# Four-layer graph kernel on one core: layer 0's one-hot matrices and gathered adjacency kept in DRAM and loaded again in layer 3, instead of being computed a second time

## The chip, the cores and the metric

One core of a Trainium2 chip runs the whole kernel. The metric is the device time of one execution in microseconds (us). Engines are named as the profile names them: PE is TensorE (PEld its weight loads), DVE is VectorE, ACT is ScalarE, POOL is GpSimd, SP is SyncE, whose queue (SPq) issues most transfers.

## What is computed

`x` is 2048 x 128, `adj` a 2048 x 2048 matrix of zeros and ones with a density of about 0.001 (some two ones in a row). Before every layer x is normalised and passed through a ReLU (`h`), and each layer's result is added to x.

```python
# layer 0: attention with 4 heads, softmax over the neighbours
e = leaky_relu(parent[:, None, :] + child[None, :, :], 0.2)
att = softmax(where(adj[..., None] > 0, e, -9e15), axis=1)
x = x + einsum('njh,jhf->nhf', att, wh).reshape(n, -1)
# layer 1: adj.T @ h, divided by the degree; layer 2: Chebyshev terms of adj, two products
# layer 3
XW = h @ W;  den = exp(leaky_relu(s_row[:, None] + s_col[None, :], 0.01))
num = adj @ den
att = where(num != 0, den / where(num != 0, num, 1), 0)
x = x + adj @ (att @ XW)
```

## The kernel before, in words

A tile is 128 of the 2048 nodes, so there are T = 16 tiles of nodes `it`, and each adjacency column block has 16 row blocks `jt`. The adjacency lies in SBUF in bf16, as `A` and turned as `AT`. Since a tile of 128 nodes has few distinct neighbours, layers 0 and 3 don't multiply by full columns: for each tile the neighbours are numbered (slots, `slotb`), in three chunks of row blocks (`CHUNKS` = 0 to 5, 6 to 12, 13 to 15), and a one-hot matrix `G` (128 x 16 x 128, bf16, 512 KB) picks them out. A matmul with G gathers the neighbours' rows, of AT among others. The adjacency gathered so is called `ATc` in layer 0 (3 chunks, 128 x 384) and `ATc3` in layer 3.

Each of these two layers first reads a flag that DVE computed (`dense`, `dense3`) and takes a branch (`choose`, L352): `by_slots`, which runs here, or `over_all`. Every engine does this by itself. The flag costs a register load and a jump.

Layer 0 by slots, per tile (`by_slots` of each engine): DVE writes G in one instruction (`one_hot`, L1517), PE gathers from it (`gather`, L1010: 48 matmuls with the node features at L1019, 16 with AT at L1021), ACT copies the two results out of PSUM (`slot_copies`, L680: wc and ATc), DVE makes 12 weight blocks `zc` out of them (`slot_weights`, L1527), PE multiplies these (`slot_output`, L1026). SP brings a row of thresholds per tile (`rows`, 256 KB, L433). G and ATc have two buffers, wc and zc four. DVE's order is one_hot(it+1), slot_weights(it).

Layers 1 and 2 are three dense products (L1059, L1081) with conversions and joins beside them. Before layer 2's last product is joined, DVE makes the first two one-hots of layer 3 (L1614, L1619) and clears a small matrix `Eb`.

Layer 3 by slots. PE works in this order for tile it (`tile3`): num3(it, 0) (L1224, L1231), u3(it-1, 0 and 1) (L1242), num3(it, 1), u3(it-1, 2 and 3), then gather3(it+2) (L1194): 16 matmuls of G3 with AT, one with Eb (which puts a one in a place of the gathered adjacency for nodes that have no neighbours), and 16 of G3 with the six columns of `rp`. ACT takes a logarithm and an exponential per quarter (L843, L845) and copies ATc3 (L851). DVE's order for tile it is one_hot3(it+2) and then, for each of four quarters c, a row block of denominators for tile it+1 (`den3`, L1736, three of them, and `own3`, L1745, in the fourth), times_y (L1754), times_own (L1761), refine (L1768); after the third quarter edges3(it+2) (L1723 to L1727), which reads what gather3(it+2) left. num3(it+1, 0) waits for all three den3 of tile it+1. So PE and DVE each have a fixed order and hand over to each other a few times per tile. All engines loop twice over buffers b = 0 and 1 (`sweep`), with the first two and last two tiles written out.

At layer 3's start PE does gather3(0), t_row(2), gather3(1), t_row(3) (a t_row, L1141, spreads a row of factors over all partitions), and ACT copies each t_row (L796) before it goes to layer 3's branch.

Of the kernel before, what the change touches and what calls it, by code (L numbers as in the profile page):

```python
# [31 lines left out]
P = 128  # L32
# [3 lines left out]
H = 4  # L36
# [24 lines left out]
def gnn_stack(nc, x, adj, w0, att0, w2, w3, a3, out):  # L61
    ctx = ExitStack()
    with ctx:
# [43 lines left out]
        ATc = [at(f"ATc_{b}", B + 39 + 0.75 * b, [P, NC, P], BF16) for b in range(2)]  # L107
        rows = [at(f"rows_{b}", B + 44 + 2 * b, [P, H * P]) for b in range(2)]
        tauT = at("tauT", B + 42.5, [T * H, P])
        tau = nc.dram_tensor("tau", (T * H, P), F32).ap()  # L110
        rest0 = at("rest0", B + 52, [P, 4, WC])
# [49 lines left out]
        Eb = at("Eb", 176, [P, T, P], BF16)  # L161
# [15 lines left out]
        def const(name, shape, dt=F32):  # L177
            size = 1
            for n in shape[1:]:
# [15 lines left out]
        mk = const("mk", [P, T])  # L195
        over3 = const("over3", [P, 1])
# [77 lines left out]
        rows_loaded = [sem(f"rows_loaded{b}") for b in range(2)]  # L274
        pc_ready = sem("pc_ready")
# [3 lines left out]
        g3_ready = sem("g3_ready")  # L279
# [3 lines left out]
        at3_ready = sem("at3_ready")  # L283
# [60 lines left out]
                  g3_used: 2, e3_copied: 2, at3_ready: 2, num3_bank: 8, acc_used: 2, t_ready: 4, att3_ready: 8, att3_used: 8, un3_kept: 2,  # L344
# [68 lines left out]
        def _(sp):  # L413
# [22 lines left out]
            choose(sp, 0, by_slots, lambda: None)  # L436
# [8 lines left out]
        def _(pool):  # L445
# [163 lines left out]
        def _(act):  # L609
# [71 lines left out]
            def slot_copies(it, b):  # L681
# [4 lines left out]
                act.wait_ge(pc_ready, it + 3)  # L686
                nc.scalar.copy(ATc[b % 2][:, :, :].rearrange("p c i -> p (c i)"),
# [13 lines left out]
            def by_slots():  # L701
                rounds(act, slot_copies, previous_output)
                copy_output(T - 1)
                act.sem_inc(bc_copied, 48)
# [100 lines left out]
            def over_all3():  # L805
                broadcast_copies(52)
# [40 lines left out]
            def edges3(it, b):  # L847

                act.wait_ge(g3_used, it + 3)
                act.wait_ge(num3_bank, 4 * it + 4)  # L850
                nc.scalar.copy(ATc3[b][:, :, :].rearrange("p c i -> p (c i)"), bank[4 + b][:, 0:NC * P]).then_inc(at3_ready, 1)  # L851

# [8 lines left out]
            def tile3(it, b):  # L861
# [4 lines left out]
                if within(it, 2):  # L866
                    edges3(it + 2, b)

            def by_slots3():
                act.wait_ge(rp_ready, 10)  # L870
                edges3(0, 0)
                edges3(1, 1)
# [8 lines left out]
        def _(pe):  # L881
# [160 lines left out]
            def by_slots():  # L1042
                pe.wait_ge(pieces0_ready, 25)
                gather(0, 0)
# [150 lines left out]
            def gather3(it, b):  # L1195


                pe.wait_ge(g3_ready, 2 * it + 2)
                pe.wait_ge(e3_copied, it + 1)
                pe.wait_ge(at3_ready, it + 1)  # L1200
                for c, (first, end) in enumerate(CHUNKS):
                    for jt in range(first, end):
                        nc.tensor.matmul(bank[4 + b][:, P * c:P * c + P], G3[b][:, jt, :],
                                         AT[:, jt, bass.ds(it * P, P)], start=jt == first, stop=jt == end - 1 and c > 0)
                    if c == 0:
                        nc.tensor.matmul(bank[4 + b][:, 0:P], Eb[:, bass.ds(it, 1), :].rearrange("p o s -> p (o s)"),
                                         identb[:, :], start=False, stop=True)
                    for jt in range(first, end):
                        last = nc.tensor.matmul(bank[4 + b][:, P * NC + 6 * c:P * NC + 6 * c + 6], G3[b][:, jt, :],
# [4 lines left out]
            def num3(it, b, p):  # L1214
# [3 lines left out]
                pe.wait_ge(at3_ready, it + 3)  # L1218
# [36 lines left out]
            def by_slots3():  # L1255
                pe.wait_ge(rp_ready, 10)
# [13 lines left out]
        def _(dve):  # L1270
# [182 lines left out]
            def finish(o):  # L1453
# [5 lines left out]
                                             ALU.subtract))  # L1459
                then(nc.vector.tensor_tensor(Os[:, :, :, :], tcol[:, :, :].unsqueeze(3).to_broadcast([P, T, H, F1]),  # L1460
# [57 lines left out]
            def one_hot(it, b):  # L1518

                dve.wait_ge(gathered, it + 1)  # L1520
                if not isinstance(it, int):
                    apart(dve)
                nc.vector.tensor_tensor(G[b % 2][:, :, :], iota[:, :].unsqueeze(1).to_broadcast([P, T, P]),  # L1523
                                        slotb[:, bass.ds(it, 1), :].rearrange("p o j -> p (o j)").unsqueeze(2)
                                        .to_broadcast([P, T, P]), ALU.is_equal).then_inc(g_ready, 1)

            def slot_weights(it, b):  # L1527
# [5 lines left out]
                for c in range(NC):  # L1533
                    for h in range(H):
                        last = nc.vector.scalar_tensor_tensor(  # L1535
                            zc[b][:, c, h, :], rows[b % 2][:, P * h:P * h + P],
                            wc[b][:, c, H * F1 + h:H * F1 + h + 1], ATc[b % 2][:, c, :], ALU.max, ALU.mult)
                last.then_inc(pc_ready, 1)

            def by_slots():  # L1540
                one_hot(0, 0)
                for it in range(T):
                    if it + 1 < T:
                        one_hot(it + 1, (it + 1) % 4)
# [64 lines left out]
            def one_hot3(it, b):  # L1609

# [224 lines left out]
```

## Time and profile before

| | us |
|---|---|
| median of 3 runs | 692.52 |
| lowest and highest | 686.78, 692.58 |
| the profiled execution, whole | 690.29 |
| its span, first to last instruction | 688.5 |

What lies around the span is 1.8 us. The page gives PE 83% busy, DVE 72%, ACT 36% and POOL 13% of the span, but these are averages over stages. By the timeline the stages are: loading and turning the adjacency up to 72 us, layer 0 by slots from 72 to 201, layers 1 and 2 up to about 376, layer 3 by slots from 376 to 652, its last dense product up to the end. Each place below is given in us from the span's start.

### The profile page before, as it was taken

To read this page: it belongs to the slowest core of one execution; us is meant where nothing else is said; L and a number is where in the kernel's file an instruction comes from. 1 tells how busy PE (TensorE), PEld (TensorE's weight loads), DVE (VectorE), ACT (ScalarE), POOL (GpSimd) and SP (SyncE) were. 2 spreads that over 40 slices of the span, in tenths; PEclk is the share of its full clock that TensorE was granted. 3 is DMA by queue.
4 is the path that set the end of the run, shared out by engine and by line. 5 is a ranking of instruction groups with operands and counts; after the bars stand their busy time and mean duration, and the time that the engine had idled before them with its cause. 6 is when DMAs were issued, how large, how long until landed. Compare 5 with 4: busy or idle time off the path is not lost.

```text
span 688.5 us, 15070 instructions
## 1 busy us (share of the span) xinstructions
PE 569.2 (83%) x5741; PEld 519.8 (76%) x5741; DVE 497.5 (72%) x1001; ACT 250.0 (36%) x401; POOL 89.0 (13%) x81
## 2 busy tenths in 40 slices
PE   1688589999902998598897499999999899999797
PEld 1577589999901565497884299999899899998697
DVE  2853498888385355446767399999999999999611
ACT  2699011121003133365544123433333333333363
POOL 1119000000010001243432000000000000002041
PEclk9995699999755999699998699999999999999999
DMA  8693111111000000000000000000000000000001
GB/s 299 262 371 144 38 48 48 34 44 46 0 1 0 1 1 0 0 1 1 1 1 2 3 1 2 2 1 0 0 0 0 0 0 0 0 1 1 0 17 46
DMA packets 8355, 24.37 MB, mean 35 GB/s; under 512 B 688, under 2 KB 3696, under 8 KB 6256
## 3 DMA queue, kind: packets, MB, share of 16 engines
q1 hardware_dynamic: 7328, 23.10, 9.3%
q10 hardware_dynamic: 976, 0.59, 0.3%
q8 instruction: 32, 0.52, 0.3%
q14 instruction: 19, 0.16, 0.1%
HBM read 22.61 MB, written 1.08 MB: 34 GB/s over the span
## 4 chain that ended last, share of the span: by engine, by line
PE 43%; DVE 17%; issue 6%; ACT 4%; POOL 1%; DVEq 0%; ACTq 0%; POOLq 0%
PE bank L1224 15%; PE bank L1081 10%; PE bank L1059 7%; PE bank L1231 4%; PE bank L1242 4%; DVE h L1345 2%; DVE denw L1736 2%; DVE dTc L1761 2%; DVE tc L1754 2%; ACT yc L843 2%; DVE yc L1768 1%; ACT yc L845 1%; PE bank L1111 1%; DVE stats L1299 1%; DVE e L1643 1%
## 5 line engine op out<-in xcount | busy, mean ns | idle before, releaser
L1224 PE MATMUL bank<-ATc,denc 128*128 128x128 f32 x1024 | 122.5, 278 | 19.5 <-DVE denw L1736 18.6
L1224 PEld LDWEIGHTS bank<-ATc,denc 128*128 128x128 f32 x1024 | 118.1, 194 | 21.9 <-issue 18.9
L1081 PE MATMUL bank<-pcs,Ar 128*128 128x256 f32 x768 | 95.1, 287 | 7.2 <-DVEq L1331 3.7
L1081 PEld LDWEIGHTS bank<-pcs,Ar 128*128 128x128 f32 x768 | 93.9, 196 | 8.8 <-DVEq L1331 4.7
L843 ACT ACTIVATE yc<-bank 128x512 f32<-128x512 f32 x64 | 37.7, 589 | 155.5 <-PE bank L1231 155.5
L537 POOL CAST Ar<-AT 128x2048 fp32r<-128x2048 bf16 x24 | 47.4, 1984 | 312.8 <-PE bank L1231 245.1
L1019 PE MATMUL bank<-whp,G 128*128 128x136 bf16 x768 | 63.1, 226 | 8.9 <-DVE G L1523 8.9
L1242 PE MATMUL bank<-XW,yc 128*128 128x128 f32 x512 | 67.0, 285 | 2.6 <-DVE yc L1768 2.6
L1059 PE MATMUL bank<-pcs,A 128*128 128x385 bf16 x256 | 45.4, 339 | 28.7 <-DVEq L1324 28.7
L1242 PEld LDWEIGHTS bank<-XW,yc 128*128 128x128 f32 x512 | 60.8, 195 | 6.7 <-DVE yc L1768 3.0
L1535 DVE SCALAR_TENSOR_TENSOR zc<-rows,wc,ATc 128x128 f32<-128x128 f32 x192 | 51.8, 347 | 18.7 <-ACT wc L685 18.7
L1019 PEld LDWEIGHTS bank<-whp,G 128*128 128x128 bf16 x768 | 56.4, 101 | 9.1 <-issue 6.1
L1059 PEld LDWEIGHTS bank<-pcs,A 128*128 x256 | 25.8, 101 | 47.8 <-issue 31.7
L1021 PE MATMUL bank<-AT,G 128*128 (+1 forms) x256 | 56.8, 222 | 0.0
L1038 PE MATMUL bank<-wc,zc 128*128 128x33 f32 x384 | 49.7, 290 | 0.9 <-ACT Oc L694 0.9
L1038 PEld LDWEIGHTS bank<-wc,zc 128*128 128x128 f32 x384 | 48.6, 208 | 1.1 <-issue 1.1
L730 ACT CAST Ar<-AT 128x2048 fp32r<-128x2048 bf16 x24 | 45.5, 1907 | 0.0
L1754 DVE TENSOR_TENSOR tc<-bank,yc 128x512 f32<-128x512 f32 x64 | 43.8, 684 | 1.9 <-ACT yc L845 1.2
L1761 DVE TENSOR_TENSOR dTc<-dTc,yc 128x512 f32<-128x512 f32 x64 | 44.7, 699 | 0.0
L1736 DVE TENSOR_SCALAR denc<-cB,rc 128x2048 f32<-128x2048 f32 x32 | 42.9, 1342 | 0.3 <-DVE rc L1727 0.3
L1768 DVE SCALAR_TENSOR_TENSOR yc<-tc,dTc 128x512 f32<-128x512 f32 x64 | 42.5, 684 | 0.0
L845 ACT ACTIVATE yc<-yc 128x512 f32<-128x512 f32 x64 | 40.4, 631 | 2.0
(202 smaller groups left out, 793.6 us busy)
## 6 DMA issues: line engine op xcount, KB each, us to landing
a<-in_adj SPq DMA_DIRECT2D x16, 1024.0 KB, 6.1
rows<-tau SPq DMA_DIRECT2D x16, 256.0 KB, 3.2
out<-X SPq DMA_DIRECT2D x4, 256.0 KB, 2.2
W<-in_L_gnn_W ACTq DMA_DIRECT2D x1, 192.0 KB, 6.5
attB<-in_L_gnn_att_weight ACTq DMA_DIRECT2D x1, 128.0 KB, 4.7
a3B<-in_L_gnn_a ACTq DMA_DIRECT2D x1, 128.0 KB, 8.9
W<-in_L_gnn_weight ACTq DMA_DIRECT2D x1, 64.0 KB, 1.9
W<-in_L_gnn_W ACTq DMA_DIRECT2D x1, 64.0 KB, 6.9
```

The costliest lines, as they stand in the source:

```text
L843: nc.scalar.activation(yc[b][c][:, :], bank[c][:, :], ACT.Ln).then_inc(ln_ready, 1)
L1019: nc.tensor.matmul(bank[b % 2][:, WC * c:WC * c + WC], G[b % 2][:, jt, :], whp[:, jt, k, :], start=jt == first and k == 0, stop=jt == end ...
L1021: last = nc.tensor.matmul(bank[2 + b % 2][:, P * c:P * c + P], G[b % 2][:, jt, :], AT[:, jt, bass.ds(it * P, P)], start=jt == first, stop= ...
L1038: last = nc.tensor.matmul(bank[7][:, F1 * h:F1 * h + F1], zc[b][:, c, h, :], wc[b][:, c, F1 * h:F1 * h + F1], start=c == 0, stop=c == NC - 1)
L1059: last = nc.tensor.matmul(bank[b][:, 0:columns], adjacency[:, kt, bass.ds((GT * q + 2 * g + b) * P, P)], pieces[:, kt, 0:columns], start=k ...
L1081: last = nc.tensor.matmul(bank[t % 2][:, 0:2 * D], Ar[t % 4][:, kt, :], pieces[:, kt, :], start=kt == 0, stop=kt == T - 1)
L1224: nc.tensor.matmul(bank[c][:, P * k:P * k + P], denc[b][:, part, j0:j0 + P], ATc3[b][:, part, :], start=k == 0 and part == 0, stop=False, ...
L1242: last = nc.tensor.matmul(bank[6 + b][:, 0:D], yc[b][c][:, P * k:P * k + P], XW[:, 4 * c + k, 0:D], start=c == 0 and k == 0, stop=c == 3 a ...
L1535: last = nc.vector.scalar_tensor_tensor(zc[b][:, c, h, :], rows[b % 2][:, P * h:P * h + P], wc[b][:, c, H * F1 + h:H * F1 + h + 1], ATc[b ...
L1736: nc.vector.tensor_scalar(den, row[:, :], rc[b][:, c, 0:1], rc[b][:, c, 1:2], ALU.mult, ALU.max).then_inc(denc_ready, 1)
L1754: nc.vector.tensor_tensor(tc[c % 2][:, :], bank[c][:, :], yc[b][c][:, :], ALU.mult).then_inc(t_ready, 1)
L1761: nc.vector.tensor_tensor(own, own, yc[b][c][:, :], ALU.mult).then_inc(yd_ready, 1)
```

## The change

In layer 0, SP stores each G (512 KB) and each ATc to DRAM (`kept_G`, `kept_A`). ATc is now f32 (192 KB instead of 96). G takes layer 3's form in layer 0 already: its last chunk is written by a second instruction, so that both halves of its 128 columns hold the same 64 slots. Therefore `slot_weights` writes only the upper half of partitions in the last chunk, and POOL clears the lower halves of the four zc buffers once, with four memsets inside its branch, for which PE waits. After layer 0, SP overwrites one row in each tile of kept_A (`lone`, 2048 single words), which takes the place of Eb. The first two one-hots are made by DVE before its branch. The two tiles that layer 3 starts with are loaded into G3 and ATc3 during the dense layers, the others inside layer 3 by SP. Layer 3's one-hots, the 17 matmuls that gathered AT, Eb and ACT's copies into ATc3 are gone.

```diff
 # SP, layer 0, per tile (rows as before, then)
+                    keep_one_hot(it)
+                    if it > 0:
+                        keep_adjacency(it - 1)
+                keep_adjacency(T - 1)
...
+            def keep_one_hot(it):
+                sp.wait_ge(g_ready, 2 * it + 2)
+                sp.dma_start(kept_G[P * it:P * it + P, :], G[it % 2][:, :, :].rearrange("p j s -> p (j s)")
+                             ).then_inc(g_kept[it % 2], 16)
+            def keep_adjacency(it):
+                sp.wait_ge(e_copied, it + 3)
+                sp.dma_start(kept_A[P * it:P * it + P, :], ATc[it % 2][:, :, :].rearrange("p c i -> p (c i)")
+                             ).then_inc(a_kept[it % 2], 16)
+            def fetch(it):
+                b = it % 2
+                if it >= 2:
+                    sp.wait_ge(g3_used, it + 1)
+                sp.dma_start(G3[b][:, :, :].rearrange("p j s -> p (j s)"), kept_G[P * it:P * it + P, :]
+                             ).then_inc(g3_loaded[b], 16)
+                if it >= 2:
+                    sp.wait_ge(num3_bank, 4 * it + 4)
+                sp.dma_start(ATc3[b][:, :, :].rearrange("p c i -> p (c i)"), kept_A[P * it:P * it + P, :]
+                             ).then_inc(a3_loaded[b], 16)
 # POOL, layer 0, inside its branch
+                for b in range(4):
+                    nc.gpsimd.memset(zc[b][0:HP, NC - 1, :, :], 0.0).then_inc(zc_zero, 1)
 # ACT, slot_copies of layer 0, ahead of the copy to ATc
+                if within(it, -2):
+                    act.wait_ge(a_kept[b % 2], 8 * (it - b % 2))
 # PE, layer 0, before its first gather
+                pe.wait_ge(zc_zero, 4)
 # PE, gather3
-                pe.wait_ge(g3_ready, 2 * it + 2)
+                pe.wait_ge(g3_loaded[b], 8 * (it - b) + 16)
                 pe.wait_ge(e3_copied, it + 1)
-                pe.wait_ge(at3_ready, it + 1)
...
-                        nc.tensor.matmul(bank[4 + b][:, P * c:P * c + P], G3[b][:, jt, :],
-                                         AT[:, jt, bass.ds(it * P, P)], start=jt == first, stop=jt == end - 1 and c > 0)
 # DVE, one_hot of layer 0
+                if it >= 2:
+                    dve.wait_ge(g_kept[it % 2], 16 * (it // 2))
 # DVE, ahead of layer 0's branch
+            dve.wait_ge(choice, 1)
+            one_hot(0, 0)
+            one_hot(1, 1)
             choose(dve, 0, *counted(by_slots, over_all))
 # DVE, tile3 of layer 3
-                if within(it, 2):
-                    one_hot3(it + 2, b)
```

How the instructions move, at the three places that matter. First PE in layer 3, the end of the order for tile 0 and the start of tile 1 (`denc`, `denw` are the denominators of num3, `AT` the adjacency). Before:

```order
L1224 MATMUL bank<-ATc_0_185,denc_159 128x128 x16
L1231 MATMUL bank<-ATc_0_185,denw_161 128x128 x8
L1203 MATMUL bank<-AT,G_0_166 128x128 x6
L1206 MATMUL bank<-identb,Eb 128x128
L1209 MATMUL bank<-rp,G_0_166 128x6 x6
L1203 MATMUL bank<-AT,G_0_166 128x128 x7
L1209 MATMUL bank<-rp,G_0_166 128x6 x7
L1203 MATMUL bank<-AT,G_0_166 128x128 x3
L1209 MATMUL bank<-rp,G_0_166 128x6 x3
L1224 MATMUL bank<-ATc_1_186,denc_160 128x128 x16
```

The same place on PE after the change:

```order
L1277 MATMUL bank<-ATc_0_184,denc_159 128x128 x16
L1284 MATMUL bank<-ATc_0_184,denw_161 128x128 x8
L1262 MATMUL bank<-rp,G_0_166 128x6 x16
L1277 MATMUL bank<-ATc_1_185,denc_160 128x128 x16
L1284 MATMUL bank<-ATc_1_185,denw_162 128x128 x8
```

Of 33 matmuls between the two num3, the 17 with 128 columns went and the 16 with six columns stayed.

Second DVE in layer 3, the end of tile 1 and the start of the loop with tile 2 (ISA rows are register work of the loop). Before:

```order
L1768 SCALAR_TENSOR_TENSOR yc_174<-tc_187,dTc_165 128x512
L1768 SCALAR_TENSOR_TENSOR yc_175<-tc_188,dTc_165 128x512
L368 UNCONDITIONAL_BRANCH
L368 ISA
L1614 ISA
L1614 TENSOR_TENSOR G_0_166<-iota,slotb 128x1664
L1619 ISA
L1619 TENSOR_TENSOR G_0_166<-iota,slotb 128x384
L1733 ISA
L1734 ISA
L1736 TENSOR_SCALAR denc_160<-cB_146,rc_198 128x2048
```

Both TENSOR_TENSOR rows that write G leave this order, in each of the 14 tiles that had them; everything else keeps its place.

Third DVE at layer 0's branch, after the change:

```order
L1504 TENSOR_SCALAR dense<-bank 128x1
L1577 TENSOR_TENSOR G_91<-iota,slotb 128x1664
L1580 TENSOR_TENSOR G_91<-iota,slotb 128x384
L1577 TENSOR_TENSOR G_92<-iota,slotb 128x1664
L1580 TENSOR_TENSOR G_92<-iota,slotb 128x384
L364 TENSOR_LOAD dense
L365 COMPARE_AND_BRANCH
```

The four instructions stand ahead of the flag's load and the jump; before, one_hot(0) and one_hot(1) were the first instructions behind the jump.

## Rows read from the trace of the kernel before

**Rows 1.** Windows: length; busy PE, PEld, DVE, ACT, POOL; clock, DMA. Tiles 0, 4, 14

```profile
395.92:408.60 12.68, 12.53 (x130) 11.95 (x130) 11.24 (x15) 3.87 (x7) 0.00 (x0) 0.89 0.01 1
...
455.84:471.67 15.83, 14.89 (x162) 14.31 (x162) 15.40 (x22) 5.42 (x10) 0.00 (x0) 1.00 0.00 0
...
614.09:629.23 15.14, 13.56 (x129) 12.88 (x129) 14.70 (x20) 4.94 (x9) 3.29 (x2) 1.00 0.00 1
```

**Rows 2.** Who waited for whom, 400 to 640 us (total, times, longest)

```profile
PE bank L1224 <- DVE denw L1736: 12.8, 13, 1.6
```

**Rows 3.** Timeline of DVE, two tiles of layer 3 (start us, us, instruction)

```profile
589.59 1.88 DVE L1614 TENSOR_TENSOR G<-iota,slotb 128x1664 bf16<-128x1664 bf16 x1
...
591.86 1.34 DVE L1736 TENSOR_SCALAR denc<-cB,rc 128x2048 f32<-128x2048 f32 x1
...
605.43 1.89 DVE L1614 TENSOR_TENSOR G<-iota,slotb 128x1664 bf16<-128x1664 bf16 x1
```

**Rows 4.** Timeline of PE, one gather3 of layer 3 and what follows

```profile
453.46 0.50 PE L1203 MATMUL bank<-AT,G 128*128 x6
...
453.85 0.29 PE L1209 MATMUL bank<-rp,G 128*128 128x6 bf16 x6
454.01 0.55 PE L1203 MATMUL bank<-AT,G 128*128 x7
...
455.84 3.83 PE L1224 MATMUL bank<-ATc,denc 128*128 128x128 f32 x32 [0.89 <-DVE denw L1736]
```

**Rows 5.** Timeline of DVE, the start of layer 3

```profile
391.61 0.16 DVE L1723 TENSOR_TENSOR rc<-last,bank 128x6 f32<-128x6 f32 x1 [9.73 <-ACT ATc L851]
...
395.01 0.81 DVE L1736 TENSOR_SCALAR denw<-qBw,rc 128x1024 f32<-128x1024 f32 x1
```

**Rows 6.** Timeline of ACT, the start of layer 3

```profile
390.14 0.59 ACT L796 COPY rB<-bank 128x512 f32<-128x512 f32 x1 [2.31 <-PE bank L1141]
391.00 0.86 ACT L851 COPY ATc<-bank 128x384 f32<-128x384 f32 x2 [0.27 <-issue]
```

**Rows 7.** Timeline of PE, the start of layer 3

```profile
381.94 0.71 PE L1203 MATMUL bank<-AT,G 128*128 128x128 bf16 x5 [3.20 <-DVE rp L1674]
...
385.15 2.05 PE L1141 MATMUL bank<-diag,ones 128*128 128x512 f32 x2
387.00 0.85 PE L1203 MATMUL bank<-AT,G 128*128 128x128 bf16 x6
...
389.00 1.10 PE L1141 MATMUL bank<-diag,ones 128*128 128x512 f32 x2
395.92 5.14 PE L1224 MATMUL bank<-ATc,denc 128*128 128x128 f32 x32 [5.82 <-DVE denw L1736]
```

**Rows 8.** Timeline of all engines, the start of layer 0

```profile
71.63 0.16 DVE L1451 TENSOR_SCALAR dense<-bank 128x1 int32<-128x1 f32 x1 [0.30 <-PE bank L980]
...
75.29 4.49 DVE L1523 TENSOR_TENSOR G<-iota,slotb 128x2048 bf16<-128x2048 bf16 x2 [3.50 <-issue]
...
77.68 0.50 PE L1019 MATMUL bank<-whp,G 128*128 128x136 bf16 x3 [6.09 <-DVE G L1523]
```

**Rows 9.** Windows of layer 0, one of ten steady microseconds

```profile
130.00:140.00 10.00, 10.00 (x139) 10.00 (x137) 8.19 (x17) 2.03 (x5) 0.00 (x0) 1.00 0.21 52
```

**Rows 10.** Timeline of DVE in layer 0

```profile
161.81 2.29 DVE L1523 TENSOR_TENSOR G<-iota,slotb 128x2048 bf16<-128x2048 bf16 x1
...
168.13 2.29 DVE L1523 TENSOR_TENSOR G<-iota,slotb 128x2048 bf16<-128x2048 bf16 x1
171.36 3.24 DVE L1535 SCALAR_TENSOR_TENSOR zc<-rows,wc,ATc 128x128 f32<-128x128 f32 x12 [0.94 <-ACT wc L685]
```

**Rows 11.** DMA issues: KB each, median us from issue to landing

```profile
a<-in_adj SPq DMA_DIRECT2D x16, 1024.0 KB, 6.1
rows<-tau SPq DMA_DIRECT2D x16, 256.0 KB, 3.2
```

**Rows 12.** Timeline of POOL at the kernel's start: one of its memsets

```profile
2.91 0.20 POOL L448 MEMSET ones<- 128x128 f32 x1 [2.41 <-issue]
```

More of the change, by code:

```diff
@@ L106, in gnn_stack @@
         wc = [at(f"wc_{b}", B + 32 + 1.75 * b, [P, NC, WC]) for b in range(4)]
-        ATc = [at(f"ATc_{b}", B + 39 + 0.75 * b, [P, NC, P], BF16) for b in range(2)]
+        ATc = [at(f"ATc_{b}", B + 39 + 1.5 * b, [P, NC, P]) for b in range(2)]
         rows = [at(f"rows_{b}", B + 44 + 2 * b, [P, H * P]) for b in range(2)]
@@ L195, in gnn_stack @@
         mk = const("mk", [P, T])
+        lone = const("lone", [P, T])
         over3 = const("over3", [P, 1])
@@ L274, in gnn_stack @@
         rows_loaded = [sem(f"rows_loaded{b}") for b in range(2)]
+        g_kept = [sem(f"g_kept{b}") for b in range(2)]
+        a_kept = [sem(f"a_kept{b}") for b in range(2)]
+        lone_ready = sem("lone_ready")
+        lone_kept = sem("lone_kept")
+        zc_zero = sem("zc_zero")
+        g3_loaded = [sem(f"g3_loaded{b}") for b in range(2)]
+        a3_loaded = [sem(f"a3_loaded{b}") for b in range(2)]
         pc_ready = sem("pc_ready")
@@ L557, in over_all3 @@
                 pool.wait_ge(logits_ready, 2)
+                for b in range(2):
+                    pool.wait_ge(g3_loaded[b], 16)
+                    pool.wait_ge(a3_loaded[b], 16)
                 pool.wait_ge(qt_ready, NG)
@@ L703, in by_slots @@
                 copy_output(T - 1)
+                for b in range(2):
+                    act.wait_ge(g_kept[b], 16 * HT)
+                    act.wait_ge(a_kept[b], 16 * HT)
                 act.sem_inc(bc_copied, 48)
@@ L805, in over_all3 @@
             def over_all3():
+                for b in range(2):
+                    act.wait_ge(g3_loaded[b], 16)
+                    act.wait_ge(a3_loaded[b], 16)
                 broadcast_copies(52)
@@ L1195, in gather3 @@
             def gather3(it, b):
-                pe.wait_ge(g3_ready, 2 * it + 2)
+                pe.wait_ge(g3_loaded[b], 8 * (it - b) + 16)
                 pe.wait_ge(e3_copied, it + 1)
-                pe.wait_ge(at3_ready, it + 1)
                 for c, (first, end) in enumerate(CHUNKS):
                     for jt in range(first, end):
-                        nc.tensor.matmul(bank[4 + b][:, P * c:P * c + P], G3[b][:, jt, :],
-                                         AT[:, jt, bass.ds(it * P, P)], start=jt == first, stop=jt == end - 1 and c > 0)
[L1205 to L1209, printed above, removed]
+                        last = nc.tensor.matmul(bank[4 + b][:, 6 * c:6 * c + 6], G3[b][:, jt, :],
                                                 rp[:, jt, :, :].rearrange("p w k -> p (w k)"),
@@ L1255, in by_slots3 @@
             def by_slots3():
-                pe.wait_ge(rp_ready, 10)
+                pe.wait_ge(rp_ready, 8)
                 gather3(0, 0)
```

100 lines of the change are left out of this document (49 added, 51 removed).

## The prediction

> **What bounds the kernel now.** I read the windows first, then the waits, then the timelines of the two engines in the windows. A steady tile of layer 3 takes 15.84 us [rows 1, 3] (on DVE from 589.59 to 605.43). In it PE has 14.89 us of work and DVE is seen busy 15.40 [rows 1]; the missing 0.4 of DVE is its own hand-over before own3, so DVE never idles there for another engine. What PE lacks is a wait for DVE: the list of waits has 12.8 us in 13 waits of num3 for denw [rows 2], one per tile, 0.89 us in the tile shown [rows 4]. So in layer 3 DVE sets the pace and PE is only 0.9 us behind it. The order of work cannot hide this: denw for tile it+1 stands behind one_hot3(it+2) in DVE's fixed order, and num3(it+1, 0) cannot start without it.
>
> In layer 0 it is the other way round. PE is busy 10.00 of 10.00 us [rows 9], DVE makes a tile each 6.3 to 6.4 us (from 161.81 to 168.13) and idles 0.9 us of it for ACT's copy, which itself waits for PE [rows 10]. Removing or adding a little on DVE is free there as long as it stays under 0.9 us.
>
> Layer 3's start is a chain of its own. DVE waits 9.73 us until 391.61 for ACT's ATc copy [rows 5]; ACT comes to that copy only at 391.00, because before its branch it must copy the fourth t_row [rows 6], and PE makes this one only after gather3(1) [rows 7]. The first num3 starts at 395.92, released by denw [rows 7].
>
> **Layer 3, steady tiles.** DVE loses the two one-hot instructions: from 589.59 to 591.86, 2.27 us [rows 3]. DVE then needs 15.84 - 2.27 = 13.57 us a tile. PE loses 17 matmuls of 128 columns. The first six and the one with Eb take from 453.46 to 453.85, 56 to 57 ns each, so 17 x 0.057 = 0.97 us. The 16 with six columns stay; six of them take 0.16 us (453.85 to 454.01), 27 ns each, 0.43 us together [rows 4]. As a check, the tile that has no gather3 has 13.56 us of PE work, 1.33 less than a steady one [rows 1], and 0.97 + 0.43 = 1.40. So PE needs 14.89 - 0.97 = 13.92 us. That is more than DVE's 13.57: PE becomes the bound, by 0.35 us, and the wait for denw should vanish. A tile falls from 15.8 to 13.9 us.
>
> The starts of num3 in tiles 1 and 14 are at 408.60 and 614.09 [rows 1], 13 tiles, 205.5 us. 13 x 13.92 = 181.0, a gain of 24.5 us. Tile 0 (12.68 us, PE busy 12.53) I leave alone: PE starts with nothing behind it, and its cost is PE and what follows from its first results. Tile 14 (15.14 us) has no one-hot or gather; there DVE comes in about 0.8 us less late, 0.8 us. Tile 15 and the end remain.
>
> Is there a hidden loop, PE to ACT to DVE to PE? The three den3 don't need a result of the running num3, except that they stand behind two times_y in DVE's order; these need num3(it, 0), whose matmuls are done some 5 us into PE's tile (3.83 us of it [rows 4]), 9 us before its end. So the hand-over has room. ACT loses a copy and is busy 5.42 of 15.8 us [rows 1].
>
> The rule on issue gaps of the Trainium skill ("TensorE: Matmul & The Clock Gate", section "Back-to-back issue gap") gives about 81 ns for each 128-column matmul in a stream with weight loads. The rows here show 57 ns, so the measurement decides. By the page's figure the 17 would be worth 1.38 us, PE would need 13.51 and DVE's 13.57 would bound, and the sum would be 13 x 0.35 = 4.6 us less.
>
> **The loads that replace the work.** Each tile of layer 3 now needs 512 KB and 192 KB. The trace has 256 KB in 3.2 us and 1024 KB in 6.1 us from issue to landing [rows 11]. SP issues G3(it+2)'s load once gather3(it) is done, at the earliest two tiles before it is needed; since it issues in order, behind the previous tile's ATc3 load, that shrinks to about one tile. A load of at most 6.1 us stands against 13.9: nothing. Without that cover it would cost up to 6 us a tile.
>
> **Layer 3's start.** ACT's copy is gone from the chain, so DVE's rc work waits for gather3(0) and for DVE's own arrival in the branch. gather3(0) starts at 381.94, released by DVE's last piece of rp, and was over by 385.15 even with its 17 wide matmuls [rows 7]. For DVE's arrival the nearest row is its jump in layer 0, 3.50 us [rows 8]: 381.9 + 3.5 = 385.4. From the first rc to the end of denw is 391.61 to 395.82, 4.2 us [rows 5], so 389.6. The other condition is the fourth t_row's copy: after a gather3(0) that ends at 383 to 384, PE needs 1.85 for a t_row, under 1 for gather3(1) and 1.1 for the last t_row [rows 7], which is 387 to 388, and ACT 0.59 [rows 6]. So num3(0, 0) starts at about 389.6 instead of 395.92, a gain of 6.3 us. Bounds: if the jump takes 0.3, as ACT's arrival did [rows 6], ACT's copy decides and the gain is 7.5; if something else holds DVE, at least the 0.9 us of ACT's two copies remains.
>
> **Layer 0's start.** The flag is ready at 71.8; DVE comes out of its jump at 75.29, and PE starts at 77.68, when the first G is written [rows 8]. Now one_hot(0) runs at 71.8 to 74.1 and the jump no longer delays it. PE is then held by its own jump (unknown, as it was waiting for DVE; between nothing and 75.3 if it is like DVE's) and by POOL's jump and four memsets. A memset of 128 elements takes 0.20 us [rows 12]; one of 512 lies between that and four times as much, so four take 0.8 to 3.2 us. PE can therefore start anywhere from 74.1 to 78.5, a gain of 3.6 to a loss of 0.8. I take 1.5, near the middle.
>
> The Trainium skill ("SBUF — State Buffer", section "SBUF: two separate sides") says that DVE and GpSimd share a pair of ports under an exclusive lock, but that a DVE operation with two SBUF inputs holds off only a GpSimd operation that reads SBUF. By that the memsets, which read nothing, run beside one_hot(1); no row here shows the two side by side, and if they did block each other PE would start no sooner than 77 and this term would be 0.7 instead of 1.5.
>
> **Layer 0, steady tiles.** DVE's one-hot is split in two, which adds nothing measurable (2.27 in layer 3's two pieces against 2.29 in one [rows 3, 10]). The stores are 704 KB a tile in 6.38 us, beside rows of 256 KB. The store of G(it) is issued 2.3 us after slot_weights(it-2) ends and must land before one_hot(it+2), about 10.5 us later; that of ATc(it) has two tiles, 12.8 us. Landing times of 3.2 to 6.1 us [rows 11] fit, even two in a row. SP's rows stand behind these waits in its queue, but they have a tile of room too. Cost: nothing; without that cover, see the last rival. ATc in f32 changes one of two inputs of the 12 zc instructions (3.24 us together [rows 10]). DVE has 0.9 us of room, 0.075 for each. The other input is f32 already, so I take nothing; if each became half as long again (0.13 us), 0.7 us a tile would appear, 10 us in all. The copy to `lone` adds 0.1 us before layer 1. The 2048 single words, Eb's clearing and the first two one-hots of layer 3 lie in the dense layers beside PE's products: nothing.
>
> **The sum.** 24.5 + 0.8 + 6.3 + 1.5 - 0.1 = 33.0 us off the profiled execution's 690.29, 657.3. The median of the runs shown is 692.52, 2.2 above that execution, and the lowest 3.5 below it, so I leave it at 657. A measurement of this kernel can tell about 1% from no change.
>
> **The rivals.** (a) The gather doesn't shrink as counted, since short matmuls after the wide ones were fed by loads hidden behind these: if the 16 took 1.5 us instead of 0.43 (94 ns each), a PE tile would be 15.0 and the gain 13 x 0.8 + 0.8 + 7.7 = 18.9: 671. For it: with a column count of six only the weight load is left. Against it: the rows of 27 ns are such a stream already. A half-way result is 664. (b) PE has less work than counted and DVE's 13.57 bounds: 652.5. For it: the difference of 0.35 us is small, and the wide matmuls in the loop carry register work. (c) The starts give nothing (DVE's jump in layer 3 is longer, POOL's memsets are late): 6.3 and 1.5 become 1 and -0.8, 664. (d) The change doesn't do what it says, because the f32 ATc lengthens layer 0 by 10 us: 667. (e) Slower: SP's one queue carries the stores, and in layer 0 the ATc copy of tile it waits for the store of tile it-2. From 12.8 us between issue and landing this wait sets the period of layer 0: half of what is above it, in each of 14 tiles. To undo 33 us it needs 2.4 us a tile, a landing 4.7 us later than 12.8, 17.5 us. The longest landing among comparable transfers is 6.1 [rows 11], and the queue would have to slow to a third. At 18 us it gives 692.
>
> **How the numbers follow.** Forecast (PE bounds layer 3, starts as counted) 0.60, its own range 653 to 661. (a) with its half-way form 0.12; (b) 0.09; (c) 0.12; (d) 0.04; (e) 0.02 with 0.01 for no change. The range takes in (b), (c) and the half-way form of (a), and the 3 us by which runs of before differ on either side: 649 to 669. All but (e) are faster by over 1%: faster 0.97, same 0.01, slower 0.02.
>
> **What would show it.** Right: the wait of num3 for denw is gone or under 0.2 us a tile; starts of num3 are 13.9 us apart; DVE is busy about 13.1 of it and has a new wait for ACT's exponential; gather3 takes 0.5 us; the first num3 starts about 8 us after gather3(0) started, where it was 14; layer 0's tile is still 6.4 us with PE full. Wrong: PE's gather over 1 us, waits for a transfer on any engine, zc instructions over 0.34 us apart in start, a layer 0 tile above 6.4, or layers 1 and 2 longer by over 1 us.

## The result, and the profile after

| | before | changed |
|---|---|---|
| median, us | 691.75 (4 runs, 686.78 to 692.58) | 659.04 (4 runs, 654.31 to 659.3) |
| the profiled execution's span | 688.5 | 657.3 |

The ratio is 0.9525 with a 95% interval of 0.9462 to 0.9588: 4.75% faster. The forecast was 657.0 in a range of 649 to 669.

The span fell by 31.2 us. Cut at the same events in both profiles, it fell here (flag is DVE's `dense`, finish its first instruction after layer 0's last output):

| stretch | before | changed | gain | forecast |
|---|---|---|---|---|
| start to flag | 71.63 | 70.94 | 0.7 | - |
| flag to finish (layer 0) | 119.23 | 120.25 | -1.0 | 1.5 |
| finish to gather3(0) (dense layers) | 191.08 | 192.13 | -1.1 | -0.1 |
| gather3(0) to num3(0) (start of layer 3) | 13.98 | 7.32 | 6.7 | 6.3 |
| num3 of tile 0 to tile 1 | 12.68 | 11.40 | 1.3 | 0 |
| tile 1 to tile 14 | 205.49 | 179.62 | 25.9 | 24.5 |
| tile 14 to tile 15 | 15.14 | 14.55 | 0.6 | 0.8 |
| tile 15 to the last product | 23.61 | 23.73 | -0.1 | 0 |
| last product to the end | 35.66 | 37.36 | -1.7 | 0 |

The windows of two tiles of layer 3 in the changed kernel, steady tile 5 and tile 14, answer to [rows 1] (length; busy PE, PEld, DVE, ACT, POOL; clock, DMA share, GB/s):

```profile
457.31:471.16 13.85, 13.85 (x150) 13.34 (x147) 13.29 (x20) 5.01 (x10) 0.00 (x0) 1.00 0.15 52
581.66:596.21 14.55, 13.54 (x135) 12.86 (x131) 14.11 (x19) 5.49 (x11) 2.72 (x2) 1.00 0.00 1
```

PE is now busy for the whole of a steady tile, 13.85 of 13.85 us, and DVE for 13.29. Before it was 14.89 of 15.83 and 15.40. The bound has moved from DVE to PE. The list of waits between 380 and 640 us says the same; [rows 2] had 12.8 us in 13 waits:

```profile
PE bank L1277 <- DVE denw L1780: 2.2, 2, 1.1
```

Two waits are left, ahead of tile 1 and ahead of tile 15. The timeline of PE around gather3, as [rows 4]:

```profile
456.91 0.55 PE L1262 MATMUL bank<-rp,G 128*128 128x6 bf16 x16
457.31 3.82 PE L1277 MATMUL bank<-ATc,denc 128*128 128x128 f32 x32
```

The 16 short matmuls take 0.40 us from start to start, where 0.43 was counted, and num3 follows with no gap. The start of layer 3 on PE, as [rows 7], and then on DVE, as [rows 5]:

```profile
384.66 2.06 PE L1201 MATMUL bank<-diag,ones 128*128 128x512 f32 x2
386.51 0.61 PE L1262 MATMUL bank<-rp,G 128*128 128x6 bf16 x16
386.98 2.06 PE L1201 MATMUL bank<-diag,ones 128*128 128x512 f32 x2
390.64 3.81 PE L1277 MATMUL bank<-ATc,denc 128*128 128x128 f32 x32 [1.60 <-ACT rB L862]
```

```profile
386.33 0.16 DVE L1767 TENSOR_TENSOR rc<-last,bank 128x6 f32<-128x6 f32 x1 [3.06 <-issue]
...
389.72 0.81 DVE L1780 TENSOR_SCALAR denw<-qBw,rc 128x1024 f32<-128x1024 f32 x1
```

DVE is held by its own jump (3.06 us in which it waits for nothing that the profile shows), no longer by ACT. PE's wait is put down to ACT's copy of a t_row, but that copy ended at 389.65 and denw at 390.53, so it was denw that came last: a wait for several semaphores is to be read with the ends beside it. The first num3 runs 3.81 us where it took 5.14 [rows 7]; PE had been idle 1.6 us before it instead of 5.8, and the granted clock, 0.73 on average in that stretch before (395.92 to 401.06), was 1.00. That holds for this pair of profiles only (tile 0, further down). The start of layer 0, as [rows 8], on DVE, POOL and PE:

```profile
71.02 1.89 DVE L1577 TENSOR_TENSOR G<-iota,slotb 128x1664 bf16<-128x1664 bf16 x1
...
75.10 0.55 DVE L1580 TENSOR_TENSOR G<-iota,slotb 128x384 bf16<-128x384 bf16 x1
```

```profile
71.92 1.91 POOL L581 MEMSET zc<- 64x512 f32 x4 [2.37 <-DVE dense L1504]
```

```profile
75.54 0.50 PE L1078 MATMUL bank<-whp,G 128*128 128x136 bf16 x3 [4.64 <-DVE G L1577]
...
79.96 0.34 PE L1078 MATMUL bank<-whp,G 128*128 128x136 bf16 x3 [0.83 <-issue]
...
88.59 0.52 PE L1078 MATMUL bank<-whp,G 128*128 128x136 bf16 x3 [3.10 <-DVE G L1580]
```

PE starts 4.60 us after the flag instead of 6.05. The first G was ready at 73.4 and the memsets at 73.8. What held PE was its own jump, which the trace shows as one instruction of 3.39 us (71.88 to 75.27):

```profile
L365 PEldq COMPARE_BRANCH  x1: 3387/3387/3387, 71.9 to 71.9; - x1
```

The memsets ran beside one_hot(0) and the first half microsecond of one_hot(1), and neither side was longer than alone: DVE's four pieces last 1.89, 0.55, 1.88 and 0.55, and the memsets take 1.91 us here and 1.91 us in inside_branch (below), where DVE stands idle beside them. By the Trainium skill ("SBUF — State Buffer", section "SBUF: two separate sides") a DVE operation with two SBUF inputs locks out only a GpSimd operation that reads SBUF; the trace agrees. Then two things eat the 1.45 us. PE pauses 0.83 us in the first gather. And before gather(2) it idles 3.10 us (2.79 before), after which the granted clock falls. These are the windows of the changed kernel there:

```profile
86.00:88.00 2.00, 0.00 (x0) 0.00 (x0) 1.97 (x3) 0.41 (x2) 0.00 (x0) 1.00 0.23 81
88.00:90.00 2.00, 1.41 (x13) 1.41 (x14) 2.00 (x8) 0.00 (x0) 0.00 (x0) 0.65 0.46 179
90.00:92.00 2.00, 2.00 (x21) 2.00 (x19) 1.96 (x8) 0.00 (x0) 0.00 (x0) 0.50 0.63 240
```

At 0.50 (1.2 GHz) gather(2) takes from 88.59 to 93.95, 5.4 us; before the change it ran at 1.00 from 89.80 to 93.54, 3.7 us. The 0.31 is work that the change gave DVE: from the first zc of slot_weights(0) to the start of gather(2) it is 82.78 to 88.59, 5.81 us, where it was 84.30 to 89.80, 5.50. The sum is 1.45 - 0.83 - 0.31 - 1.6 = -1.3 us; the first slot_output comes 1.1 us later after the flag, and the table has -1.0. The 1.6 of it are this pair of profiles' and not surely the change's: the clock fell there in the second profile of the kernel before as well (before_again, below). The DMA issues, as [rows 11]:

```profile
kept_G<-G SPq DMA_DIRECT2D x16, 512.0 KB, 2.6
G<-kept_G SPq DMA_DIRECT2D x16, 512.0 KB, 3.6
rows<-tau SPq DMA_DIRECT2D x16, 256.0 KB, 3.2
kept_A<-ATc SPq DMA_DIRECT2D x16, 192.0 KB, 2.6
ATc<-kept_A SPq DMA_DIRECT2D x16, 192.0 KB, 2.3
...
kept_A<-lone SPq DMA_DIRECT2D x1, 8.0 KB, 14.5
```

Stores and loads of whole tiles land in 2.3 to 3.6 us. No engine that computes waits for one; SP's own queue does once, for 1.5 us, before it stores `lone`.

### The profile page after: what moved, and what is told of

Read it like the earlier page. It is cut to its first block, busy times and chain, and to the rows that moved or that the text cites. A ratio compares the mean times of both kernels' runs of the same rounds, so it can differ in the third digit from the quotient of the medians.

```text
span 657.3 us, 14300 instructions
## 1 busy us (share of the span) xinstructions
PE 555.5 (85%) x5469; PEld 507.6 (77%) x5469; DVE 462.1 (70%) x984; ACT 242.2 (37%) x385; POOL 89.6 (14%) x85
## 4 chain that ended last, share of the span: by engine, by line
PE 52%; DVE 10%; issue 4%; ACT 2%; POOL 1%; DVEq 0%; ACTq 0%; POOLq 0%
PE bank L1277 16%; PE bank L1141 13%; PE bank L1295 8%; PE bank L1119 7%; PE bank L1284 5%; DVE h L1398 1%; PE bank L1171 1%; PE bank L1262 1%; DVE stats L1352 1%; DVE dTc L1805 1%; PE bank L1201 1%; DVE pcs L1383 1%; PE bank L1160 1%; DVE yc L1812 0%; DVE denw L1780 0%
## 5 line engine op out<-in xcount | busy, mean ns | idle before, releaser
L1277 PE MATMUL bank<-ATc,denc 128*128 128x128 f32 x1024 | 121.1, 276 | 3.8 <-DVE denw L1780 2.2
L1141 PE MATMUL bank<-pcs,Ar 128*128 128x256 f32 x768 | 99.0, 294 | 7.1 <-DVEq L1384 3.7
L1141 PEld LDWEIGHTS bank<-pcs,Ar 128*128 128x128 f32 x768 | 97.9, 202 | 8.7 <-DVEq L1384 4.6
L595 POOL CAST Ar<-AT 128x2048 fp32r<-128x2048 bf16 x24 | 46.0, 1925 | 283.5 <-PE bank L1284 211.3
L1594 DVE SCALAR_TENSOR_TENSOR zc<-rows,wc,ATc 128x128 f32<-128x128 f32 (+1 forms) x192 | 53.6, 350 | 18.9 <-ACT wc L746 11.5
```

The costliest lines, as they stand in the source:

```text
L595: nc.gpsimd.tensor_copy(Ar[t % 4][:, :, :], AT[:, :, t * P:t * P + P]).then_inc(ar_even, 1)
L1141: last = nc.tensor.matmul(bank[t % 2][:, 0:2 * D], Ar[t % 4][:, kt, :], pieces[:, kt, :], start=kt == 0, stop=kt == T - 1)
L1277: nc.tensor.matmul(bank[c][:, P * k:P * k + P], denc[b][:, part, j0:j0 + P], ATc3[b][:, part, :], start=k == 0 and part == 0, stop=False, ...
L1594: last = nc.vector.scalar_tensor_tensor(zc[b][ps, c, h, :], rows[b % 2][ps, P * h:P * h + P], wc[b][ps, c, H * F1 + h:H * F1 + h + 1], ATc ...
```

## The experiments

**only_one_hots.** G3 comes from DRAM; PE still gathers the adjacency, with Eb and ACT's copies, and ATc3 isn't loaded.

```diff
 # gather3, before each chunk's short matmuls
+                        nc.tensor.matmul(bank[4 + b][:, P * c:P * c + P], G3[b][:, jt, :],
+                                         AT[:, jt, bass.ds(it * P, P)], start=jt == first, stop=jt == end - 1 and c > 0)
 # ACT, tile3
+                if within(it, 2):
+                    edges3(it + 2, b)
...
```

> Half of the change in layer 3: G3 comes from DRAM, but PE still gathers the adjacency (17 matmuls of 128 columns a tile), Eb is back and ACT copies ATc3. Layer 0 stays as in the changed kernel. Theory (PE's own work bounds layer 3 once DVE has lost its one-hots): starts of num3 are 14.8 to 14.9 us apart, DVE waits for ACT, num3 no longer waits for denw; layer 3's start is late again by 5 to 6 us, because ACT's copies stand before edges3 again; whole run 659 + 13 x 1.0 + 1 + 6 = 679. Rival (DVE's 13.6 us and the hand-overs bound, and PE's gather is hidden in them): starts stay 13.8 apart, and the run comes to 665.

Measured: 675.59 us (4 runs, 670.64 to 679.57), ratio 0.9758 (0.9689 to 0.9827). A steady tile, starts of num3 as its edges:

```profile
456.08:470.82 14.74, 14.74 (x161) 14.24 (x162) 13.12 (x20) 5.42 (x10) 0.00 (x0) 1.00 0.12 36
```

PE is full, 14.74 us, and DVE waits. The mean of the 13 tiles is 14.80 us. From gather3(0) to num3(0) it is 13.84 us again. The theory holds, the rival (13.8 us a tile) falls; the profiled execution took 679.57 us (679 expected), and the median is 4 us lower, as much as executions of one kernel differ by. Layer 3's start is worth 13.84 - 7.32 = 6.5 us. There the two kernels differ by the 17 matmuls and ACT's copies, and it is the copy that DVE's rc work waits for, as before the change:

```profile
393.30 0.16 DVE L1786 TENSOR_TENSOR rc<-last,bank 128x6 f32<-128x6 f32 x1 [9.59 <-ACT ATc L919]
```

**only_adjacency.** ATc3 comes from DRAM, PE's 17 matmuls are gone, and DVE makes the one-hots again; G3 isn't loaded.

```diff
             def tile3(it, b):
+                if within(it, 2):
+                    one_hot3(it + 2, b)
...
```

> The other half: ATc3 comes from DRAM and PE's 17 matmuls are gone, but DVE makes the one-hots of layer 3 again, two instructions a tile (2.27 us). Layer 0 stays as in the changed kernel. Theory (DVE bound layer 3 before, so removing PE's work alone gives nothing in the steady tiles): starts of num3 are 15.8 us apart and num3 waits about 1.8 us a tile for denw, the start of layer 3 keeps its 6 us gain; run 691.8 - 6.5 + 1 = 685 to 686. Rival (PE's matmuls were part of the loop): 14.9 apart, 673.

Measured: 681.31 us (4 runs, 675.81 to 689.84), ratio 0.9846 (0.9752 to 0.9939). A steady tile, and the waits from 395 to 600 us:

```profile
441.14:456.88 15.74, 13.94 (x145) 13.36 (x145) 15.31 (x22) 4.99 (x10) 0.00 (x0) 1.00 0.04 12
```

```profile
PE bank L1275 <- DVE denw L1795: 17.7, 13, 2.0
```

Taking 1 us of PE's work away alone leaves the tile at 15.80 us in the mean of 13 (15.81 before) and only lengthens PE's wait, from 1.0 to 1.4 us. Start of layer 3: 7.33 us, with the gain. So of the 2.0 us a tile, DVE's part alone brings 1.0 (15.81 to 14.80), PE's part alone nothing, and PE's part on top of DVE's another 1.0 (14.80 to 13.82). The run came out some 4 us below the 685 expected. Its profile (678.44 us) had dense layers of 186.07 us, 5 below the kernel before; that stretch varies so without a change (before_again, below).

**double_loads.** Every G3 from tile 2 on is loaded twice, one load after the other.

```diff
-                sp.dma_start(G3[b][:, :, :].rearrange("p j s -> p (j s)"), kept_G[P * it:P * it + P, :]
-                             ).then_inc(g3_loaded[b], 16)
+                for _ in range(2 if it >= 2 else 1):
+                    sp.dma_start(G3[b][:, :, :].rearrange("p j s -> p (j s)"), kept_G[P * it:P * it + P, :]
+                                 ).then_inc(g3_loaded[b], 16)
+                    if it >= 2:
+                        sp.wait_ge(g3_loaded[b], 32 * (it // 2) + 16 * _ + 16)
...
 # PE, gather3
-                pe.wait_ge(g3_loaded[b], 8 * (it - b) + 16)
+                pe.wait_ge(g3_loaded[b], 16 * (it - b) + 32)
```

> Each G3 from tile 2 on is loaded twice, the second load after the first has landed, so the load takes some 7 us instead of 3.6 and SP's queue is held meanwhile. Theory (the loads have over a tile of cover): starts of num3 stay 13.8 us apart, no engine waits for a transfer, time as the changed kernel (654 to 660). Rival (loads are only just hidden, or their traffic slows something): 1 to 3 us a tile appear, 670 or more.

Measured: 658.15 us in one run. Starts of num3 are 13.8 to 13.9 us apart, as in the changed kernel. The 30 issues land in 3.4 us in the median:

```profile
G<-kept_G SPq DMA_DIRECT2D x30, 512.0 KB, 3.4
```

There are some 7 us of loading G3 per tile now and still nobody waits for it: the loads have at least that much cover.

**inside_branch.** The first two one-hots go back behind DVE's jump.

```diff
-            dve.wait_ge(choice, 1)
-            one_hot(0, 0)
-            one_hot(1, 1)
             choose(dve, 0, *counted(by_slots, over_all))
 # and by_slots begins with them
```

> The first two one-hots go back behind DVE's jump; all else is the changed kernel. Theory: DVE comes out of its jump 3.5 us after the flag, the first G is ready 5.8 us after the flag, PE starts 5.9 to 6.0 us after it instead of 4.6, 1.3 us later. Rival: the first gather is then no longer crossed by the stores' traffic, or PE's idle gap before gather(2) falls otherwise, and the end of layer 0 is no later than now, or earlier. By the theory 660, by the rival 658 or less; the place to look is the time from the flag to the last slot_output.

Measured: 661.46 us (4 runs, 660.67 to 662.74), ratio 0.9579 (0.953 to 0.9628). PE starts 6.51 us after the flag, 1.9 later than in the changed kernel, but flag to finish is 120.29 us against 120.25. There is no pause in gather(0), and before gather(2) it has the same wait and, behind it, the same low clock:

```profile
77.47 0.50 PE L1078 MATMUL bank<-whp,G 128*128 128x136 bf16 x3 [6.55 <-DVE G L1580]
89.83 0.35 PE L1078 MATMUL bank<-whp,G 128*128 128x136 bf16 x3 [3.10 <-DVE G L1580]
```

```profile
92.00:94.00 2.00, 2.00 (x21) 2.00 (x20) 1.97 (x5) 0.00 (x0) 0.00 (x0) 0.50 0.25 87
```

That layer 0 ends at the same time doesn't mean that the earlier one-hots are worth nothing. The first slot_output starts 24.25 us after the flag here and 23.01 in the changed kernel:

```profile
95.21 2.82 PE L1097 MATMUL bank<-wc,zc 128*128 128x33 f32 x24
```

```profile
93.95 2.82 PE L1097 MATMUL bank<-wc,zc 128*128 128x33 f32 x24
```

The first row is inside_branch, the second the changed kernel. The 13 tiles behind it take 83.0 us in every profile of every kernel here. The last three outputs with what follows take 13.0 us here against 14.2, and they vary by as much in the kernel before (14.3 and 13.0 in its two profiles). So the earlier one-hots do bring 1.2 us, as this run's theory said, and the end of the layer hid it in this pair. The timed runs agree with that (661.46 against 658.4 to 659.0) but don't decide it: the intervals of the ratios overlap.

**changed_again, late_stores, earlier_one_hot**, side by side with the kernel before on one chip. In late_stores SP issues the stores of G(0) and G(1) after gather(0); in earlier_one_hot DVE's order in layer 0 shifts by one:

```diff
 # late_stores
-                    keep_one_hot(it)
+                    if it == 1:
+                        sp.wait_ge(gathered, 3)
+                        keep_one_hot(0)
+                        keep_one_hot(1)
+                    if it > 1:
+                        keep_one_hot(it)
 # earlier_one_hot
-                    if 0 < it < T - 1:
-                        one_hot(it + 1, (it + 1) % 4)
+                    if it < T - 2:
+                        one_hot(it + 2, (it + 2) % 4)
                     slot_weights(it, it % 4)
```

> The changed kernel itself once more, as the measure beside the next two: 654 to 660 by every theory.

> SP issues the stores of the first two one-hots only after gather(0), at about 82 instead of 73.4 and 75.7. Theory (the 0.83 us in which PE waits in gather(0) for nothing that the profile shows is the fetch of its instructions behind the stores' packets, DMA being 0.90 busy then): that pause is gone or under 0.3 us and PE reaches the end of gather(0) 0.8 us sooner; whole run 0 to 1 us less. Rival (the pause belongs to the jump alone and only shows because PE starts sooner): it stays at 79 to 80.

> In layer 0 DVE makes one_hot(it+2) ahead of slot_weights(it) instead of one_hot(it+1). Theory (PE's idle 3.1 us before gather(2), and gather(2) then at half of the clock, come from one_hot(2) standing behind slot_weights(0)): the wait is gone, the granted clock stays 1.00 there, layer 0 ends 4 to 4.7 us earlier after the flag, and the run is 654 to 655 against 659. Rival (steady tiles lose it again, since slot_weights starts later behind an earlier one-hot and DVE has only 0.6 us to spare): no change, 658 to 660, with tiles of 6.39 us and a new wait elsewhere.

| | median of 6 runs | lowest to highest | ratio to before | flag to finish |
|---|---|---|---|---|
| changed_again | 658.38 | 655.66 to 662.82 | 0.9564 (0.952 to 0.9608) | 119.75 |
| late_stores | 659.44 | 651.15 to 660.48 | 0.9536 (0.9486 to 0.9586) | 118.59 |
| earlier_one_hot | 655.55 | 648.14 to 658.17 | 0.9508 (0.9469 to 0.9547) | 115.21 |

late_stores has no pause in gather(0), as its theory said. But five profiles have the changed kernel's layer 0 (the two of it, only_one_hots, only_adjacency, double_loads), and the pause was 0.83, 0.37 and 0.73 us in three of them and absent in two, with the stores going out as early. Nor was the DMA share 0.90 in the pause: that is the window from 76 to 78, and the pause lay between 79.1 and 80.0, where it was 0.24. So that the stores delay PE's instructions is not shown; whichever it is, the time doesn't show it.

earlier_one_hot has neither the wait before gather(2) nor the low clock, and from flag to finish it takes 4.5 to 5 us less than the two profiles of the changed kernel (3 to 5 less than all five with its layer 0). These are its windows there:

```profile
88.00:90.00 2.00, 2.00 (x31) 2.00 (x28) 2.00 (x3) 0.63 (x2) 0.00 (x0) 1.00 0.43 162
90.00:92.00 2.00, 2.00 (x21) 2.00 (x21) 2.00 (x8) 0.25 (x1) 0.00 (x0) 1.00 0.81 318
```

**before_again, before_earlier, earlier_again.** The kernel before; the kernel before with the same shift; the shifted changed kernel once more.

> The kernel before once more, for a second profile: which of its stages vary from one execution to the next. If the dense layers differ by 5 us between executions of one kernel (186 or 191 us from layer 0's finish to layer 3's first gather, as the changed kernel shows), the one microsecond that the changed kernel seemed to lose there is no effect of the change. And if its last product takes 35.7 us again while the changed kernel's takes 37 to 38.5, that loss belongs to the change.

> The kernel before with the same shift as earlier_one_hot: in layer 0 DVE makes one_hot(it+2) ahead of slot_weights(it), nothing else. Theory (the gap before gather(2) was there before the change too, 2.8 us): PE's wait goes, from flag to finish 119.2 becomes 116 to 116.5, run 2.8 us less, 686 against 689. Rival (that gap belongs to the changed kernel's earlier start): under 1 us.

> The changed kernel with the shifted one-hots again, for a firmer number: 3 to 4.7 us below the changed kernel's 658 to 659, flag to finish 115.2 us again. If the first result was chance in which execution caught fewer stretches of half clock, it comes out at 657 to 659.

before_again took 690.51 us in one run. Its last product took 37.14 us, where the first profile had 35.66 and all the changed kernels 37.1 to 38.5; so the 1.7 us of the table is not the change's. From finish to gather3(0) it had 191.23 us; the changed kernel had 192.13 in one profile and 186.08 in the other. The dense layers vary by 6 us between executions of one kernel, and the table's -1.1 there says nothing. before_earlier came to 688.31 us (12 runs), ratio 0.9978 (0.9945 to 1.0011): from flag to finish 116.72 against 119.23 and 119.70. In before_again the granted clock fell at gather(2) too, after the same 2.79 us of waiting as in the first profile, where it held; these are its windows there:

```profile
89.00:91.00 2.00, 2.00 (x27) 2.00 (x25) 2.00 (x8) 0.00 (x0) 0.00 (x0) 0.66 0.03 8
91.00:93.00 2.00, 2.00 (x21) 2.00 (x19) 2.00 (x3) 0.00 (x0) 0.00 (x0) 0.50 0.22 56
```

So the gap was there before the change, and the fall behind it comes in either kernel. In before_earlier the shift takes 2.5 to 3 us off layer 0 in the profile, but the timed runs can't tell the difference from none, and by the time alone the rival (under 1 us) isn't refuted. earlier_again came to 654.29 us (6 runs, 651.94 to 656.18), ratio 0.9509 (0.9472 to 0.9547), flag to finish 115.18. The two series of the shifted kernel agree: 3 to 5 us under the changed kernel's 658.4 to 659.0, and by the ratios 1 to 4 us. The intervals of its ratio and of the changed kernel's still overlap.

**Layer 0 and tile 0 over all profiles.** Times from the flag in us; the last column is from the third last slot_output to finish:

| | PE starts | gather(2) | first slot_output | last three outputs | finish |
|---|---|---|---|---|---|
| before | 6.05 | 18.17 | 21.91 | 14.3 | 119.23 |
| before_again | 6.53 | 18.34 | 23.71 | 13.0 | 119.70 |
| changed | 4.60 | 17.65 | 23.01 | 14.2 | 120.25 |
| changed_again | 4.98 | 17.48 | 22.86 | 13.9 | 119.75 |
| only_one_hots | 4.91 | 17.92 | 23.30 | 14.1 | 120.40 |
| only_adjacency | 4.68 | 17.89 | 21.63 | 13.8 | 118.43 |
| double_loads | 4.59 | 16.94 | 22.31 | 13.0 | 118.36 |
| inside_branch | 6.51 | 18.87 | 24.25 | 13.0 | 120.29 |

The granted clock stayed at 1.00 behind gather(2)'s wait in `before` and only_adjacency and fell in the others. Like with like, the change brings the first slot_output forward by 0.3 us (21.91 to 21.63) where the clock stayed and by 0.4 to 1.4 where it fell. In the means of finish nothing of it is left: 119.5 us in the two profiles of before, 119.4 in the five of the changed layer 0.

Tile 0 of layer 3 varies in the same way. These are its windows in the changed kernel, in late_stores and in before_again:

```profile
390.64:402.04 11.40, 10.25 (x113) 9.67 (x113) 8.97 (x13) 3.92 (x7) 0.00 (x0) 1.00 0.06 17
388.80:402.91 14.11, 12.97 (x112) 12.39 (x112) 8.96 (x13) 3.91 (x7) 0.00 (x0) 0.80 0.04 8
394.71:408.71 14.00, 13.85 (x130) 13.28 (x130) 11.25 (x15) 3.87 (x7) 0.00 (x0) 0.80 0.00 1
```

late_stores has the changed kernel's layer 3 and waits 1.56 us before num3(0), as the changed kernel does with 1.60; yet the clock stood at 0.50 for the first 4 us of its tile. double_loads and inside_branch took 14.1 and 14.2 us at 0.80 and 0.79, the five others with the short wait 11.40 at 1.00. With the 5.8 us wait it was 12.7 to 14.1 in four profiles. At the same clock of 0.80, tile 0 takes 14.0 us with and 14.1 without gather3's wide matmuls in it: what PE saves there it spends waiting for DVE ahead of tile 1 (1.15 us).

## Why the prediction was right

The forecast's case happened, PE as the bound of layer 3, and by its steps:

- **DVE's pace in layer 3.** Counted: 2.27 us off DVE, 0.97 off PE, new tile 13.92. Measured 13.82 in the mean of 13 tiles, and 13.82 in the second profile too. only_adjacency shows that DVE was the bound before, only_one_hots that PE takes its place as soon as DVE is lighter. The gain over the 13 tiles was 25.9 instead of 24.5, 0.1 us a tile. It lies in the 14.89 us that were counted as PE's work before: only_one_hots runs the same matmuls in a tile and, with PE as the bound, takes 14.80. So PE was busy 14.89 by the profile but had 14.80 of work; the 0.97 for the 17 matmuls came out as 0.98.
- **57 ns against 81 ns for a wide matmul.** The rows decided it rightly: 16 short matmuls 0.40 us, the 17 wide ones 0.98 (only_one_hots' 14.80 less 13.82, 58 ns each). The Trainium skill's 81 ns ("TensorE: Matmul & The Clock Gate", section "Back-to-back issue gap") would have made DVE the bound, rival (b); instead PE fills the tile, and DVE is busy for 13.29 of its 13.85 us. (a) fell with it.
- **Layer 3's start.** Forecast 6.3, measured 6.7, and by only_one_hots 6.5. The jump, taken over from layer 0 at 3.50 us, was 3.06. Rival (c) falls for this half.
- **Tile 0** was put at no gain and brought 1.3 us in this pair of profiles. That is the clock and not the work: at a clock of 0.80 it takes 14.0 us in the kernel before (before_again) and 14.1 with the change (late_stores). Full clock came in five of eight profiles with the shorter wait ahead of num3(0) and in none of four with the longer one, which suggests that the shorter wait helps; three profiles in which it didn't, with 1.5 to 1.7 us of wait, show that it doesn't decide.
- **Layer 0's start**, forecast 1.5 us, is the term that was mis-sized. PE did start 1.5 us earlier (1.45 in this pair), held by its own jump as the step allowed, but that step took the start of PE for the gain. At the first slot_output 0.3 us are left where the clock stayed in both kernels, and over all profiles layer 0 ends 119.4 us after the flag against 119.5. What the step overlooked stood in the trace: PE waits for one_hot(2) behind slot_weights(0) anyway, and the change lengthens that piece of DVE's work by 0.3 us. inside_branch shows the early one-hots to bring 1.2 us there, earlier_one_hot that taking the wait away brings 3 to 5.
- **Layer 0's steady tiles** stayed at 6.39 us, so f32 in ATc costs no time there: zc on 128 partitions takes 347 ns as before, starts 0.26 us apart. The one third on 64 partitions takes 358, and its first starts 0.36 us after the last on 128. From the first zc of a tile to the one-hot behind it is 3.39 us instead of 3.15, and the split one-hot takes 2.28 instead of 2.21: these are the 0.3 us above, which the prediction put at nothing. In the steady tiles it does no harm: DVE's wait for ACT's copy shrinks there from 0.9 to 1.0 us to 0.6 to 0.7. Rivals (d) and (e) fall: stores land in 2.6 us where 12.8 were free.
- **Layers 1 and 2** came out 1.05 us longer, just past the sign set for being wrong. It is no effect of the change: the second profile of the changed kernel has 5 us less there.
- **The sum.** What repeats is 25.9 + 0.6 + 6.7 = 33.2 us, all of it in layer 3, against 33.0 forecast. That the two are so close is partly luck: layer 3's tiles gave 1.4 us more than forecast, and layer 0's start, put at 1.5, gave about nothing. The profiled span fell by 31.2, since 1.0 to 1.7 us were lost in each of three stretches that vary by as much without a change. Two of the rivals' times were added up a little wrongly: by its own terms (c) comes to 665 and (e) at a landing of 18 us to 694. Nothing hangs on either.

## What to carry to other kernels

When one engine is full and another nearly so, work the second one's load out before removing anything from the first: here the 2.27 us taken from DVE would have given 1.0 us a tile without the 0.97 us taken from PE, and those 0.97 alone nothing. A round trip through DRAM beats recomputing on the busiest engine where, as here, the DMA engines are idle and the loads have a tile of cover. An earlier start is worth only what is left of it behind the next wait; follow the chain to there, and read the gain at that place. A gain of a microsecond in a stretch where the granted clock moves needs several profiles of both kernels: one pair gave 1.3 us for tile 0 and -1.0 for layer 0, and neither was the change's.

## What the runs showed of the hardware that was not expected

- The granted clock fell to 0.50 (1.2 GHz) for 3 to 4 us after PE had been idle 3.09 to 3.10 us before gather(2) in both profiles of the changed kernel and in those of inside_branch, late_stores, only_one_hots and double_loads, but stayed at 1.00 (2.4 GHz) after 3.09 us in only_adjacency. After 2.79 us in the kernel before it stayed in one profile and fell in the other. So the length of the gap alone doesn't say whether it falls, and the change isn't shown to cause it. The fall cost 1.6 us in the one gather. Nor does it ahead of num3(0): after waits of 1.5 to 2.0 us tile 0 ran at 1.00 in five profiles and at 0.80 on average in three.
- PE's jump at layer 0's branch took 3.4 to 4.0 us in all twelve profiles, one instruction in the trace. DVE came out of its own 3.1 to 4.0 us after its last instruction, wherever nothing else held it longer.
- On DVE, the first of the instructions on 64 partitions started 0.36 us after the last on 128, where neighbours of one shape start 0.26 us apart.
- The same kernel's executions differ by 5 to 6 us in the dense layers (186.08 and 192.13 us for one kernel), which is more than most of the single terms above; the cut at events in the profile tells apart what the whole time can't.
- Storing 2048 single words took 14.5 us for 8 KB, where a store of 512 KB took 2.6 and a load 3.6. It lay beside the dense layers.
- Four memsets of 64 x 512 words on POOL took 1.91 us together, 0.5 us each, beside DVE's one-hots and, in inside_branch, with DVE idle.
